# Low parts of the picked tables: one subtraction over eight row blocks in place of two over four

## What is computed

```
e = jnp.stack([tbl_0[ids[:, 0]], ..., tbl_31[ids[:, 31]]], axis=1)   # (512, 32, 128)
dot = jnp.einsum('bnd,bmd->bnm', e, e)
z = dot[:, iu, ju]                                   # the pairs above the diagonal
h = jnp.concatenate([z, dense_ctx], axis=1)
h = jnp.maximum(h @ W_top1 + b_top1, 0.0)            # 512 outputs
h = jnp.maximum(h @ W_top2 + b_top2, 0.0)            # 256 outputs
y = h @ W_top3                                       # 1 output
```

## Time and profile before

| | us |
|---|---|
| median of 3 runs | 123.6 |
| lowest and highest | 123.24 and 124.68 |
| the profiled execution, whole | 123.41 |
| its span in the trace | 121.6 |
| PE busy | 109.9 (90%) |
| ACT busy | 77.6 (64%) |
| DVE busy | 75.2 (62%) |
| POOL busy | 69.8 (57%) |

### The profile page before, as it was taken

How to read it: one execution, slowest core, us unless ns; L and a number is a source line. 1 busy time by engine, 2 the same in 40 slices (tenths; PEclk the granted TensorE clock), 3 DMA queues, 4 the chain that set the end, 5 groups by cost and what they waited for, 6 DMA issues and landing times.

```text
span 121.6 us, 2668 instructions
## 1 busy us (share of the span) xinstructions
PE 109.9 (90%) x1024; PEld 93.3 (77%) x1024; DVE 75.2 (62%) x196; ACT 77.6 (64%) x78; POOL 69.8 (57%) x76
## 2 busy tenths in 40 slices
PE   0397599999999999999999999999879999999992
PEld 0354488888888888888688787999779989989870
DVE  0989999999999997999993900242401251134211
ACT  4179989999999999999999974304321032100231
POOL 2777678777776777777777777777765000000000
PEclk9999999999999999999999999999999999999999
DMA  3895767656675578467695211255848320242000
GB/s 100 240 338 191 225 253 251 212 175 217 256 265 196 161 273 299 120 253 263 148 362 175 65 46 43 58 128 154 241 138 251 89 68 0 53 153 59 0 0 1
DMA packets 11150, 19.81 MB, mean 163 GB/s; under 512 B 2353, under 2 KB 7473, under 8 KB 11138
## 3 DMA queue, kind: packets, MB, share of 16 engines
q1 hardware_dynamic: 7522, 13.74, 34.9%
q0 software_dynamic: 2176, 4.46, 12.6%
q10 hardware_dynamic: 1440, 1.44, 3.5%
HBM read 17.54 MB, written 2.13 MB: 162 GB/s over the span
## 4 chain that ended last, share of the span: by engine, by line
PE 69%; ACT 10%; DMA 7%; DVE 6%; issue 3%; ACTq 2%; SPq 1%
PE two_ps L552 20%; PE two_ps L554 19%; PE two_ps L613 10%; ACT onehot L433 5%; PE free_ps L594 4%; DMA home<-picked 4%; PE free_ps L624 4%; PE turn_ps L562 3%; ACT emb L412 3%; DMA dot_out<-home 3%; PE two_ps L594 3%; PE two_ps L624 2%; DVE onehot L323 2%; DVE narrow L333 2%; PE two_ps L629 2%
## 5 line engine op out<-in xcount | busy, mean ns | idle before, releaser
L304 POOL DMA_INDIRECT rows<-tables,row_no x64 | 65.0, 1016 | 19.9 <-issue 11.0
L552 PE MATMUL two_ps<-onehot,high 128*128 128x512 f32 x128 | 52.7, 412 | 7.5 <-DVE low L313 7.2
L554 PE MATMUL two_ps<-onehot,low 128*128 128x512 f32 x128 | 51.0, 399 | 0.0
L433 ACT ACTIVATE onehot<-narrow 128x2560 fp32r<-128x2560 f16 (+3 forms) x16 | 35.6, 2240 | 0.4 <-PE two_ps L554 0.4
L552 PEld LDWEIGHTS two_ps<-onehot,high 128*128 128x128 f32 x128 | 24.7, 193 | 14.5 <-issue 5.7
L554 PEld LDWEIGHTS two_ps<-onehot,low 128*128 128x128 f32 x128 | 24.8, 194 | 4.7
L313 DVE TENSOR_TENSOR low<-home,high 128x512 fp32r<-128x512 f32 (+1 forms) x36 | 22.3, 623 | 3.6 <-issue 2.9
L323 DVE TENSOR_SCALAR onehot<-pick_id,own_row 128x512 fp32r<-128x512 int16 x53 | 23.0, 481 | 0.0
L333 DVE TENSOR_SCALAR narrow<-pick_id,own_row 128x512 f16<-128x512 int16 x75 | 22.6, 364 | 0.0
L412 ACT ACTIVATE high<-home 128x1024 fp32r<-128x1024 f32 (+2 forms) x18 | 17.7, 991 | 3.4 <-DMA home<-picked 3.4
L412 ACT ACTIVATE emb<-turn_ps 128x512 f32<-128x512 f32 (+2 forms) x20 | 11.5, 591 | 9.0 <-PE turn_ps L562 6.0
(11 more groups left out here) (35 smaller groups left out, 49.9 us busy)
## 6 DMA issues: line engine op xcount, KB each, us to landing
home<-picked SPq DMA_DIRECT2D x10, 512.0 KB, 3.6
home<-picked SPq DMA_DIRECT2D x4, 640.0 KB, 3.9
pick_id<-pick_ids SPq DMA_DIRECT2D x13, 128.0 KB, 3.8
w_sb<-w SPq DMA_DIRECT2D x3, 512.0 KB, 5.5
dot_out<-home SPq DMA_DIRECT2D x10, 128.0 KB, 2.6
rows<-tables,row_no POOLq DMA_INDIRECT x64, 3.5
dot_out<-home ACTq DMA_DIRECT2D x6, 128.0 KB, 2.5
pairs<-dot_out SPq DMA_DIRECT2D x10, 64.0 KB, 1.9
```

What stands on the lines that cost most here:

```text
L304: pool.indirect_dma_start(rows[:, k % ROWS_HELD, i, :], None, lone if one_table else tables, bass.IndirectOffsetOnAxis(ap=id_sb[:, 0, c:c ...
L433: act.activation(onehot[:, at:at + n, :], narrow[:, t % 2, n0:n0 + n, :], ACT.Copy).then_inc(onehot_act, n)
L552: pe.matmul(out, high[:, at, D * k:D * (k + 1)], onehot[:, c % HOT, :], start=(k == 0), stop=False)
L554: pe.matmul(out, low[:, at, D * k:D * (k + 1)], onehot[:, c % HOT, :], start=False, stop=(k == KR[t] - 1)).then_inc(picked_done, 1)
```

## The change

The sizes of the low pieces go from 4, 4, 2 row blocks to 8, 2. A piece of four blocks is a subtraction over 512 elements in each partition, one of eight over 1024.

```
-LOW_CUT, HOT_CUT = [4, 4, 2], [3]
+LOW_CUT, HOT_CUT = [8, 2], [3]
```

## The result

| | before | after |
|---|---|---|
| median, us | 123.42 | 130.36 |
| lowest and highest, us | 122.61 and 124.68 | 128.68 and 132.22 |
| profiled execution, us | 123.41 | 132.22 |
| its span, us | 121.6 | 130.4 |

The ratio of after to before is 1.044, with a 95% interval of 1.032 to 1.056; it is taken over undisturbed runs, which leaves the longest ones out. The changed kernel is slower by 5 to 7 us. Forecast was 124.1.

What follows compares the result with a forecast made beforehand. PE and ACT were taken as full side by side through the picking, with PE idle before table 1. The profiled 123.41 us plus 0.54 for table 1's late start gave 123.95, 124.1 as median; range 123.5 to 124.8.

Steps and rivals of the forecast that it cites:

- it too moves by 0.54: POOL's gathers, from gather 8 at 15.02: they start 0.54 us later, like PE and ACT, so the three queues keep their distances.
- The sum: Whole kernel: 123.41 us profiled plus 0.54 for table 1's late start is 123.95; 124.1 on the scale of the median.
- The rival with POOL: Picking phase: gathers wait for a subtraction's end, each up to 0.54 us longer, at most 7.6; up to 131; chance 0.03.
- The rival with the clock: Before table 1: PE's idle time grows to 2.26 us, its clock falls, 1.9 us lost, time 126.0; chance 0.05.
- The range: Whole kernel: 123.5 to 124.8 us, from the swallowed case with its scatter to above the forecast's own.
- the two slower rivals: PE's clock falling before table 1 (126.0 us, 0.05) and subtractions holding up POOL's gathers (up to 131, 0.03); together 0.08.

Runs made afterwards that it cites:

- the filler with late transposes: Changed kernel plus 12 transposes of a constant on PE ahead of table 1, and transposes of gathered rows one table later: 124.23 us, ratio 0.999.
- the early table 1 without wide pieces: Kernel before with table 1's first low piece ahead of table 2's narrow matrices: 123.00, again 123.08 us; with gathered-row transposes one table later: 123.08, again 122.88.
- filler alone: Changed kernel plus 12 transposes of a constant on PE between tables 0 and 1: 130.76 us.
- early table 1 with wide pieces: Kernel before with table 1's first low piece early, gathered-row transposes one table later, pieces of 8 and 2 from table 2 on: 124.62 us, ratio 1.006.

## Why the prediction was wrong

**Right.** The wide subtraction takes what was put for it, 1220 ns where 1.22 us was forecast:

```profile
L313 DVE TENSOR_TENSOR low<-home,high 128x1024 fp32r<-128x1024 f32 x14 | 17.1, 1220 | 5.9 <-issue 5.9
```

PE starts table 1 at 14.02 (forecast 14.09), with 2.25 us of idle time (2.26). No later table waits for a low part. DVE is busy 0.9 us less (0.8), and it is worth nothing.

**The step that failed** is "it too moves by 0.54", said of POOL. The sum has no term for gathers that take longer, and takes their 0.95 us as something that the change leaves alone. On tables 2 to 14 it asked whether the low part and the one-hot matrices still come in time for PE, and they do. It did not ask what the longer instruction and the new order on DVE do to POOL. In place of that nothing, the gathers' mean went from 1025 to 1289 ns, PE waited 5.0 us for rows, and the clock fell twice, for 3.4 us of delay.

**The rival with POOL was right in the main, and was put down by a row that does not bear on it.** It had the mechanism (a gather waits for the end of a subtraction), the loss (slower, up to 131) and its size: 7.6 us at most, where 6.7 us of hold under running subtractions were found between 15 and 75 us. It did not have the second hold, and its place was only partly right: rows are late at 54.98 already, not only at tile 14. It got a chance of 0.03, by gather 47, which took 0.94 us beside a subtraction. But that gather began at 66.59 and the subtraction at 66.61: the gather was first, so the row says nothing on a gather that begins in a running one. Both kinds of hold were in the trace of before. Three of its early gathers, and DVE beside them:

```profile
17.69 1.61 POOL L304 DMA_INDIRECT rows<-tables,row_no  x1 [0.30 <-PE two_ps L554]
19.61 1.49 POOL L304 DMA_INDIRECT rows<-tables,row_no  x1 [0.31 <-PE two_ps L554]
21.41 1.00 POOL L304 DMA_INDIRECT rows<-tables,row_no  x1 [0.30 <-PE two_ps L554]
```

```profile
17.79 1.39 DVE L333 TENSOR_SCALAR narrow<-pick_id,own_row 128x512 f16<-128x512 int16 x5
19.11 0.68 DVE L313 TENSOR_TENSOR low<-home,high 128x512 fp32r<-128x512 f32 x1
...
20.90 0.68 DVE L313 TENSOR_TENSOR low<-home,high 128x512 fp32r<-128x512 f32 x1
```

Each begins 0.5 us into a subtraction of 512 elements. The third has the first hold alone: its subtraction ends at 21.58, the gather 0.83 us later, at 22.41. The first two are held again; they end at 19.30 and 21.10, 0.19 and 0.20 us after the next subtraction starts.

The Trainium skill, SBUF — State Buffer, says in its section on who interferes with whom that `tensor_scalar` in a 2-port mode takes the port pair that GpSimd needs to write a transfer's descriptors, and that `tensor_tensor` with both inputs in SBUF holds up GpSimd's reads; it adds, as inferred, that `tensor_tensor` leaves the writing of descriptors alone. The traces agree that a running `tensor_tensor` holds something that a gather needs at its start: 1.76 us in place of 0.94. That it is this port pair, and a read of the row numbers, no run here shows; the runs show the order of events alone.

**The rival with the clock** had 0.05 and happened too. The profile of before looked safe (1.72 us of idle time, no fall), but it was one execution. With the wide pieces from table 2 on, the clock fell behind 1.63 us, less than that. And of 25 runs of the kernel before, 9 show a mean granted clock of 0.986 or less, which is one fall (3.4 us at half, of 123) or more, and all nine took 124.36 us or longer. No trace of these runs was kept, so where the clock fell in them is not shown; it looks as if the gap of before was already at the edge. With the gap closed, by the filler with late transposes (10 runs) or by the early table 1 without wide pieces (39 runs), no run reads under 0.998. Where rows were late or nearly so behind a closed gap (filler alone, early table 1 with wide pieces), 4 of 14 read 0.985 to 0.987: the clock then fell somewhere else.

**The range** rested on a sum of 0.5 us, with the two slower rivals at 0.08 together. The loss was 5 to 7, and both of them were in it. The clock fell twice in the profile, at 1.6 and 1.8 us of delay, each near the 1.9 put for one.

## What to carry to other kernels

An order on one engine can be another's timetable: before two instructions are joined or moved, see which transfers and which other engine run in between, not only who waits for their results. Where POOL issues gathers, a longer DVE instruction is a longer hold for each gather that begins in it; such a wait is in no list of waits, and shows as a gather's own duration. When one row seems to rule a mechanism out, look which of the two began first. And where rows may come late, give their reader a table of slack: it cost nothing here and took away most of the loss.

## What the runs showed of the hardware

A gather instruction of 0.94 us on POOL that begins while a DVE instruction is running, a subtraction included, does not end before that instruction has ended and 0.81 us or more have passed: so for all 262 that began in a subtraction with over 0.13 us left. One that begins just before a subtraction runs beside it in 0.94.

Some of the gathers held in this way are held once more, up to 3.60 us in all. Of the 14 in the changed kernel that took over 1.3 us between 15 and 75 us, seven ended 0.20 us after the start of the third one-hot instruction (which for all seven is only 0.09 to 0.10 us later than the first hold alone would give), four 0.19 to 0.21 us after the start of a subtraction, two while DVE was idle (one of these, that of 59.39, with the first hold alone) and one beside a narrow instruction. Yet other gathers ran to their end in a row of narrow instructions without this: that of 34.27 in the changed kernel took 1.05 us. What decides it is open. So is why the same order of instructions now locks into gathers of 0.95 to 1.00 and now of 1.5 us.
